# Attention probabilities turned in 32x32 blocks on VectorE and moved between partitions by transfers, instead of turned on TensorE, in a two-layer graph network on one core

## The reference

```python
def _L0_gnn_ref(X, A, W, a):
    h = jnp.einsum('bnf,fo->bno', X, W)
    att_self = jnp.einsum('bno,od->bnd', h, a[0])
    att_neigh = jnp.einsum('bno,od->bnd', h, a[1])
    e = jax.nn.leaky_relu(att_self + jnp.swapaxes(att_neigh, 1, 2), ALPHA)
    e = e + NEG * (1.0 - adj)[None, :, :]
    alpha = jax.nn.softmax(e, axis=-1)
    return jnp.concatenate([jnp.einsum('bij,bjo->bio', alpha, h), h], axis=-1)

def _L1_gnn_ref(h, adj, Wq, bq, Wk, bk, Wv, bv, Wo, bo):
    q, k, v = (split_heads(h @ W.T + b) for W, b in ((Wq, bq), (Wk, bk), (Wv, bv)))
    scores = jnp.einsum('bhqd,bhkd->bhqk', q, k) * scale
    scores = jnp.where((adj == 0)[None, None, :, :], -jnp.inf, scores)
    attn = jax.nn.softmax(scores, axis=-1)
    out = jnp.einsum('bhqk,bhkd->bhqd', attn, v).transpose(0, 2, 1, 3).reshape(b, n, D_MODEL)
    return out @ Wo.T + bo

x = _layernorm(x + _L0_gnn_ref(x, adj, ...), axis=-1)
x = _layernorm(x + _L1_gnn_ref(x, adj, ...), axis=-1)
```

## Time and profile before

| | |
|---|---|
| median of three runs | 3468.7 us (3466.77 to 3469.16) |
| the profiled execution: its time, its span | 3468.5 us, 3466.6 us |
| busy: TensorE, its weight loads | 3412.3 us (98%), 2903.8 us (84%) |
| busy: VectorE, ScalarE, GpSimd | 2688.1 us (78%), 2510.2 us (72%), 1616.8 us (47%) |
| transfers | 111.19 MB, 396 issues, all from SyncE's queue; 9.6% of the engines' time |
| granted clock of TensorE, mean over the span | 0.995 |

### The profile page before, as it was taken

How to read it: one execution, slowest core, us unless ns; L and a number is a source line. 1 busy time by engine, 2 the same in 40 slices (tenths; PEclk the granted TensorE clock), 3 DMA queues, 4 the chain that set the end, 5 groups by cost and what they waited for, 6 DMA issues and landing times.

```text
span 3466.6 us, 65791 instructions
## 1 busy us (share of the span) xinstructions
PE 3412.3 (98%) x23168; PEld 2903.8 (84%) x23168; DVE 2688.1 (78%) x7607; ACT 2510.2 (72%) x5382; POOL 1616.8 (47%) x1542
## 2 busy tenths in 40 slices
PE   6999999999999999999999999999999999999998
PEld 5888888888888888888888888888888888888886
DVE  5787777877777877778777778777787777877776
ACT  4776777776777767777777777677777777777775
POOL 2544454445454444544454544445444454444443
PEclk8999999999999999999999999999999999999999
DMA  3000011000111010110001110001100011100100
GB/s 128 19 22 28 25 38 38 31 26 22 34 38 38 20 31 25 37 38 31 26 21 36 38 35 22 26 31 38 38 25 32 19 38 37 32 25 25 31 13 25
DMA packets 59652, 111.19 MB, mean 32 GB/s; under 512 B 6720, under 2 KB 7488, under 8 KB 59328
## 3 DMA queue, kind: packets, MB, share of 16 engines
q1 hardware_dynamic: 59328, 106.99, 9.6%
HBM read 73.41 MB, written 33.55 MB: 31 GB/s over the span
## 4 chain that ended last, share of the span: by engine, by line
PE 97%; DVE 1%; ACT 1%; issue 0%; DMA 0%; POOL 0%; SPq 0%; ACTq 0%; DVEq 0%; POOLq 0%
PE R_bank L541 47%; PE O_bank L629 14%; PE T_bank L613 14%; PE S_bank L603 13%; PE L_bank L541 5%; PE L_bank L532 3%; PE L_bank L556 0%; DMA prob<-WkT 0%; POOL turned L985 0%; DVE prob L900 0%; PE O_bank L541 0%; DMA alpha<-a 0%; ACT tokens L674 0%; DVE n_wide L946 0%; ACT prob L734 0%
## 5 line engine op out<-in xcount | busy, mean ns | idle before, releaser
L965 POOL TENSOR_TENSOR prob<-prob,rsum 128x512 f32<-128x512 f32 x1024 | 1059.5, 1041 | 1309.3 <-DVE rsum L906 1307.4
L734 ACT ACTIVATE prob<-prob,negmax 128x512 f32<-128x512 f32 x1024 | 739.6, 722 | 323.3 <-DVE negmax L900 314.9
L659 ACT ACTIVATE probT<-T_bank 128x512 fp32r<-128x512 f32 x1024 | 579.0, 594 | 220.8 <-PE T_bank L613 214.6
L900 DVE CUSTOM_DVE_ANT_0 prob<-S_bank,mask 128x512 f32<-128x512 f32 x1024 | 695.5, 679 | 2.2 <-PE S_bank L603 1.1
L794 DVE TENSOR_TENSOR probT<-T_bank,probT 128x512 fp32r<-128x512 f32 x1024 | 675.9, 683 | 5.1 <-ACT probT L659 3.1
L613 PE MATMUL T_bank<-ident,prob 128*128 128x128 f32 x4096 | 597.7, 276 | 3.1 <-DVE probT L794 3.1
L629 PE MATMUL O_bank<-probT,v_st 128*128 128x256 f32 x4096 | 586.6, 288 | 2.8 <-DVE probT L794 2.8
L906 DVE RECIPROCAL rsum<-psum_row 128x1 f32<-128x1 f32 x1024 | 164.9, 161 | 542.7 <-PE S_bank L603 303.4
L613 PEld LDWEIGHTS T_bank<-ident,prob 128*128 128x128 f32 x4096 | 459.0, 141 | 106.1 <-issue 93.8
L629 PEld LDWEIGHTS O_bank<-probT,v_st 128*128 128x128 f32 x4096 | 522.2, 190 | 21.5 <-issue 11.5
L603 PE MATMUL S_bank<-qk_pair 64*128 64x512 f32 x3072 | 494.1, 426 | 2.5 <-DVE negmax L900 2.2
(11 more groups left out here) (84 smaller groups left out, 4374.0 us busy)
## 6 DMA issues: line engine op xcount, KB each, us to landing
tokens<-xT SPq DMA_DIRECT2D x128, 256.0 KB, 3.0
tokens<-x SPq DMA_DIRECT2D x128, 256.0 KB, 2.7
out<-tokens SPq DMA_DIRECT2D x128, 256.0 KB, 2.1
tokens<-adj SPq DMA_DIRECT2D x1, 1024.0 KB, 6.5
tokens<-WqT SPq DMA_DIRECT2D x1, 1024.0 KB, 5.5
prob<-WkT SPq DMA_DIRECT2D x1, 1024.0 KB, 7.9
tokens<-WvT SPq DMA_DIRECT2D x1, 1024.0 KB, 6.5
prob<-WoT SPq DMA_DIRECT2D x1, 1024.0 KB, 5.0
```

Source lines behind the costliest of these rows:

```text
L659: act.activation(dst, src, ACT.Copy).then_inc(done, 1)
L734: act.activation(prob[:, slot, :], prob[:, slot, :], ACT.Exp, bias=negmax[:, slot:slot + 1], scale=-1.0, accum_out=psum_row[:, slot:slot + ...
L900: dve.tensor_tensor_reduce(prob[:, slot, :], S_bank[s % 2][:, :], mask[:, s % 8 // 2, :], -SCALE, HUGE, ALU.add, ALU.min, negmax[:, slot:s ...
L965: pool.tensor_tensor(prob[:, slot, :], prob[:, slot, :], rsum[:, slot:slot + 1].to_broadcast([P, N]), ALU.mult).then_inc(p_norm, 1)
```

## The change

The step `turn` on TensorE and T_bank are gone. Four tiles (two heads x two query tiles: a phase, 8 a graph) are written to one of three buffers of `prob` in such a layout that 16 blocks of 32x32 of each are turned in place on VectorE (`vt`). Then 16 transfers a phase (4 words `mv`, each 4 transfers) carry the blocks from 32 partitions to 32 others into `turned_lo_prob` (two buffers); each moves 32 partitions x 4 x 128 elements, 64 KB. ScalarE writes the HI half from there to `turned_hi_prob` (one buffer) and GpSimd the LO half in place. The sums read four runs of 64 columns. Of four normalisations one is on ScalarE (`norm`), three on GpSimd (`pnorm`); the inversion is a word of its own (`inv`). Scores have three banks in turn, L_bank has two; O_bank is for weighted sums only. `qk_pair`, `turned` and `alpha` have one buffer instead of two, and N is read from its bank, without a copy. All five tables are new.

```diff
-SLOTS = 4
-HALVES = 3
+SLOTS = 12
 TENSOR_PLAN = (
-    "weigh scores turn turn",
-    "weigh k1 N scores",
+    "scores k1 N",
+    "weigh weigh scores",
+    "scores O0 C0",
...
-        turned = sb("turned", [P, 2, 2, C, P], F32R)
+        turned = sb("turned", [P, 2, C, P], F32R)
-        qk_pair = sb("qk_pair", [P, 2, 4, N], F32R)
+        qk_pair = sb("qk_pair", [P, 4, N], F32R)
-        prob = sb("prob", [P, SLOTS, N])
-        probT = sb("probT", [P, HALVES, 2, T, 2 * P], F32R)
+        prob = sb("prob", [P, 3, 4 * T, 4, BLK])
+        turned_lo_prob = sb("turned_lo_prob", [P, 2, 4, T, P], F32R)
+        turned_hi_prob = sb("turned_hi_prob", [P, 4, T, P], F32R)
-        S_bank = [bank(f"S_bank{i}") for i in range(2)]
-        T_bank = [bank(f"T_bank{i}") for i in range(2)]
+        S_bank = [bank(f"S_bank{i}") for i in range(3)]
-        L_bank = bank("L_bank")
+        L_bank = [bank(f"L_bank{i}") for i in range(2)]
...
+            def move_probs(R, m):
+                ph, a = m // 4, m % 4
+                if a == 0:
+                    sp.wait_ge(p_turned, R.n(32, 4 * ph + 4))
+                own = slice(BLK * a, BLK * (a + 1))
+                for d in range(4):
+                    sp.dma_start(turned_lo_prob[BLK * d:BLK * (d + 1), ph % 2, a, :, :].bitcast(F32),
+                                 prob[own, prob_buffer(R, ph), d::4, :, :].rearrange("p c j i -> p c (j i)")).then_inc(p_moved[prob_buffer(R, ph)][a], 16)
...
-                if due(R.n(32, 2 * u)):
-                    pe.wait_ge(s_red, R.n(32, 2 * u))
+                if due(R.n(32, 2 * u - 1)):
+                    pe.wait_ge(s_red, R.n(32, 2 * u - 1))
...
-            def turn_probs(R, s):
-                pe.wait_ge(p_norm, R.n(32, s + 1))
-                if due(R.n(16, s // 2)):
-                    pe.wait_ge(t_lo[s % 2], R.n(16, s // 2))
-                for c in range(T):
-                    last = pe.transpose(T_bank[s % 2][:, c * P:(c + 1) * P], prob[:, s % SLOTS, c * P:(c + 1) * P],
-                                        ident[:, :])
-                last.then_inc(t_mm, 1)
             def weigh(R, g):
-                pe.wait_ge(t_lo[w], R.n(16, 4 * pair + 2 * half + 2))
+                pe.wait_ge(p_lo, R.n(32, 4 * ph + 4))
...
-                    last = pe.matmul(O_bank[:, o_cols(w)], v_st[:, c, (2 * pair + w) % HEADS, :],
-                                     probT[:, half_buffer(R, g), s, c, :], start=(c, s) == todo[0], stop=(c, s) == todo[-1])
+                    probs = (turned_hi_prob[:, :, c, DH * w:DH * (w + 1)],
+                             turned_lo_prob[:, ph % 2, :, c, DH * w:DH * (w + 1)])[s]
...
             def qk_of_pair_hi(R, pair):
-                if due(R.n(32, 8 * (pair - 1))):
-                    act.wait_ge(s_mm, R.n(32, 8 * (pair - 1)))
+                if due(R.n(32, 8 * pair)):
+                    act.wait_ge(s_mm, R.n(32, 8 * pair))
...
+            def normalise_last(R, p):
+                s = 4 * p + 3
+                act.wait_ge(p_inv, R.n(32, s + 1))
+                act.activation(prob_tile(R, s), prob_tile(R, s), ACT.Copy,
+                               scale=rsum[:, slot_of(R, s):slot_of(R, s) + 1]).then_inc(p_normed_act, 1)
+            def probs_hi(R, m):
+                ph, a = m // 4, m % 4
+                if a == 0 and due(R.n(16, 2 * ph)):
+                    act.wait_ge(pv_mm, R.n(16, 2 * ph))
+                act.wait_ge(p_moved[prob_buffer(R, ph)][a], moved_count(R, ph))
+                split_hi(turned_hi_prob[:, a, :, :], turned_lo_prob[:, ph % 2, a, :, :].bitcast(F32), p_hi)
...
             def reduce_scores(R, s):
-                if due(R.n(32, s - SLOTS + 1)):
-                    dve.wait_ge(t_mm, R.n(32, s - SLOTS + 1))
+                if s % 4 == 0 and due(R.n(8, s // 4 - 2)):
+                    for a in range(4):
+                        dve.wait_ge(p_moved[prob_buffer(R, s // 4)][a], moved_count(R, s // 4 - 3))
...
+            def turn_blocks(R, s):
+                if s % 4 == 3:
+                    if due(R.n(16, s // 2 - 3)):
+                        dve.wait_ge(pv_mm, R.n(16, s // 2 - 3))
+                    dve.wait_ge(p_normed_act, R.n(8, s // 4 + 1))
+                else:
+                    dve.wait_ge(p_normed_pool, R.n(24, 3 * (s // 4) + s % 4 + 1))
+                dve.transpose(prob_tile(R, s), prob_tile(R, s)).then_inc(p_turned, 1)
...
+            def probs_lo(R, m):
+                ph, a = m // 4, m % 4
+                pool.wait_ge(p_hi, R.n(32, m + 1))
+                pool.tensor_tensor(turned_lo_prob[:, ph % 2, a, :, :], turned_lo_prob[:, ph % 2, a, :, :].bitcast(F32),
+                                   turned_hi_prob[:, a, :, :].bitcast(F32), ALU.subtract).then_inc(p_lo, 1)
```

479 lines of the change are left out of this document (244 added, 235 removed).

## The result

The changed kernel takes 3536.1 us (median of four executions, 3528.5 to 3546.8) against 3468.9 (3466.8 to 3471.1): a ratio of 1.020, 95% interval 1.017 to 1.022. It is slower by about 2%, where 3180 was forecast. The profiled execution took 3528.5 us, its span 3526.7; it is the fastest of the four, and the experiments are compared with it. The four lie within 18 us, so a difference of less than that from a single run is not read as one.

The account below looks back on a forecast made before the run. TensorE was taken as the bound: 106.1 - 14.1 = 92.0 us a round, plus 4.45 of waits, 96.5. Head 216.9 + 29 rounds (2798.5) + tail 162.9 = 3178.3, and 1.9 around it: 3180 us; range 3050 to 3330.

Parts of the forecast that it names:

- SyncE's queue: Issuing the moves, loads and stores: 0.48 us each, 128 x 0.48 + 12 x 0.48 = 67 us a round.
- The limit beside it: SyncE's issue cost from which its queue would decide the time: (106.1 - 5.8) / 128 = 0.78 us an issue.
- The prediction's own sign of being wrong: Among the signs: an engine other than TensorE has the largest share of the chain.
- Slower: Rival: issuing the moves on SyncE's in-order queue becomes the bound; at 0.80 an issue, 108.2 a round, 3540 us; chance 0.09.
- What leaves TensorE: Removing 32 turns of 0.44 us takes 14.1 us from TensorE's round, 106.1 to 92.0.
- the waits: TensorE's waits for sums, scores, q and k tiles and late ScalarE: 4.45 us a round, making it 96.5.
- no change of the clock: TensorE's granted clock stays at 1.00, the upper level, since it keeps nearly all its work in every stretch.
- Transposes: VectorE's 32 transposes of 128x512 a round: 0.66 us each, leaving VectorE at about 83.5 us.
- GpSimd: 32 lo halves at 1.29 us in, 8 of 32 normalisations at 1.04 out: 50.4 becomes 83.4 us a round.
- Weighted sums: TensorE's sums with four runs of 64 columns: priced at nothing; upper bound 1.2 us a round.
- The landing: Time for a move to land, counted in the head's first phase: 2.1 us.
- Head and tail: Before and after the 29 rounds: 216.9 and 162.9 us, with turns removed and 9.8 for moves added in each.

Follow-up runs that it names:

- twelve issues: Changed kernel with the same bytes in 12 transfers a phase instead of 16 (48, 48 and 32 partitions), tokens not put where they belong: 3203.6 us.
- spare issues: Changed kernel with 8 moves a phase instead of 16, plus 8 tiny transfers nobody waits for: 3373.2 us with these behind the moves, 3722.7 ahead of them.
- four issues: Changed kernel with the same bytes in 4 transfers a phase instead of 16, each straight across 128 partitions, so blocks stay on their partitions: 3194.1 us.
- both edges open: Changed kernel with four buffers for the probabilities instead of three, and ScalarE's hi halves reading a constant tile without waiting for moves: 3445.2 us.
- spare issues behind: Changed kernel with 8 straight moves a phase instead of 16, followed by 8 tiny transfers that nothing waits for: 3373.2 us.

## Why the prediction was wrong

**The step that failed** is SyncE's queue: "128 x 0.48 + 12 x 0.48 = 67 us", and from it that it would hide, "it decides from (106.1 - 5.8) / 128 = 0.78 us an issue". The term was mis-sized: an issue of a move takes 0.64, and loads and stores among them 0.59, so 128 x 0.64 + 12 x 0.59 = 89 us a round; with the few issues that take up to 1.9 us it is the 92.9 worked out above. At the assumed size (twelve issues, 7.7 us a phase) the runs give 3203.6 us and a round of 96.50, at the true one 3528 and 106.8. The 0.48 came from loads out of the chip's memory, which were the only issues back to back in the trace of before; it should have carried both its ends, up to the 0.80 of the same rows, into the range.

The limit beside it was wrong too. The queue decides at 0.64, when it has 89 us in a round of 96.5, and not only at the 0.78 that fills it. The sum compared averages over a round. But a phase's sixteen issues and their landing, 16 x 0.64 + 2.0 = 12.2 us, lie between the phase's last transpose and its weighted sums, as long as a whole phase lasts on average (96.5 / 8 = 12.1). The prediction had this path in the head and the tail, 9.8 us each, and nothing for it in the 29 rounds. Where phases are bunched, the queue is the only thing on the chain for 35.7 us on end, and a queue that is over 92% full has little to catch up in afterwards. The spare issues show that both count: 176 us with the moves in front of them, and 349.5 more behind them. With one division, 89 / 96.5, I would have forecast 3180 again. The prediction's own sign of being wrong came: an owner other than TensorE, SyncE's queue with 45%, has the largest share of the chain. The rival "Slower" named the right queue, with a chance of 0.09. That its 3540 is nearly the measured time is luck: it comes from 0.80 us an issue and a queue that is never idle, and the runs show 0.64 and 14 us of idle time a round.

**What leaves TensorE** was nearly right: matmuls for turns are gone, and the round without queue is 96.2 to 96.5 us. The 29 rounds of the changed kernel and then those with four issues, with busy us of each engine and, behind POOL's, the clock, answer to the earlier trace rows:

```profile
243.07:3341.46 3098.39, 2805.08 (x17284) 2291.91 (x17283) 2444.61 (x6842) 2396.67 (x5104) 2412.89 (x2088) 0.97 0.40 109
```
```profile
228.11:3021.60 2793.49, 2719.79 (x17288) 2231.19 (x17286) 2439.90 (x6845) 2384.25 (x5106) 2402.74 (x2088) 1.00 0.39 121
```

With four issues TensorE is busy, by the modelled ends of its matmuls, for 2719.79 / 29 = 93.8 us of a round and idle for 2.5; 92.0 and 4.45 were forecast. The sum came out, but 12.3 us left TensorE and not 14.1, and the waits are smaller by about as much: that the round is right to 0.2 us is in part luck. In the changed kernel it is busy for 96.7 us and idle for 10.1. So of the 10.5 us that a round is longer, 7.6 are idle time and 2.9 are the same matmuls taking longer, at a mean granted clock of 0.97, where the other has 1.00, the upper level (2.4 GHz). The prediction had argued for no change of the clock from a TensorE that keeps nearly all its work; with 10 us of idle time in a round that condition was gone. How much of the 2.9 lies on the path of the loss isn't shown.

**Transposes** at 0.66: 0.686, right. The 1.24 that I estimated from the figure of the Trainium skill, page "VectorE: DVE Perf Modes", section "The three transpose paths", did not come. **GpSimd**: lo halves 1.29 as priced, normalisations 1.08 for 1.04. **Weighted sums** with four runs of columns cost nothing that shows: with four issues their matmuls take 295 and 285 ns in the mean, before the change 288. **The landing**, 2.1 forecast, is 2.0.

**Head and tail**: 216.9 and 162.9 were forecast; with twelve issues they are 229.1 and 174.2 (3201.8 - 3027.59), together 23.5 us more, which is all of what separates 3203.6 from 3180. In the changed kernel they are 243.1 and 185.2. Why the head doesn't shrink by the 19.8 us of its turns was not tried.

**Open**: how the loss of 334 us splits between the straight path to the sums and the late loads once ScalarE's 77 us are gone. Whether loads and stores issued from another queue would give back the second part was not tried. The kernel with both edges open (3445) still lies 72 us above the one with spare issues behind (3373), which has a shorter path and other transfers.

## What to carry to other kernels

Price a queue twice: its issues in a round against the round, and the issues between a producer's last instruction and its consumer's first against the slack of that path, which is what a bunch of sixteen small transfers spends; and where the producer bunches its phases, price the queue over the bunch and not over the round. Where many small transfers replace an engine's work, count issues before bytes: 325 to 334 us hung here on sixteen against four, eight or twelve issues of the same bytes, and two passes through the chip's memory with ten issues won 4.6% over the kernel before, where the direct moves lost 2%. Be wary of handing issues to a computing engine whose own results the transfer waits for: the one attempt here took 3807 us.
